# A residual add on GpSimd, one gather later in every step

## The reference

```python
xn = _layernorm(x, axis=-1)
x = x + _L0_attn_ref(xn, Wq, Wk, Wv, Wo, We) + _L0_ffn_ref(xn, gate_w, w1, b1, w2, b2)

# _L0_attn_ref: ctx = X @ We.T ; influence = ctx @ ctx.T
scores = jnp.einsum('bqhd,bkhd->bhqk', Q, K) * SCALE + 0.1 * influence[:, None]
out = softmax(scores) @ V, heads joined, then @ Wo.T

# _L0_ffn_ref: probabilities by softmax over 8 logits, top 2 taken
h = gelu(w1[e] @ x + b1[e])
y = w2[e] @ h + b2[e]
out = sum over the 2 experts of y * prob
```

## Time and profile before

| | us |
|---|---|
| median of 3 runs | 795.96 |
| lowest and highest run | 795.24 and 799.38 |
| the profiled execution's own time | 795.8 |
| its span, from first to last instruction | 794.1 |
| second attention in the span | about 552 to the end |

### The profile page before, as it was taken

One profiled execution on the slowest core, in us unless ns is written; L12 is line 12 of the kernel. 1 busy time (PEld: TensorE's weight loads), 2 busy tenths in 40 slices (PEclk: granted clock), 3 DMA queues, 4 the chain that ended last, 5 costly groups with the idle time before them and its releaser, 6 DMA issues.

```text
span 794.1 us, 25470 instructions
## 1 busy us (share of the span) xinstructions
PE 694.2 (87%) x8124; PEld 454.6 (57%) x8124; DVE 657.5 (83%) x1182; ACT 527.1 (66%) x1128; POOL 536.6 (68%) x600
## 2 busy tenths in 40 slices
PE   0477889898899897889999999999899999999984
PEld 0363344444444453479999999998444444544442
DVE  8989868887778785879999999999888888888851
ACT  2591566776667676767777777777677767667663
POOL 9660656666466565137777777876777777877885
PEclk9995789999999998999999999999999999999998
DMA  9669545666465564643333333332667776776652
GB/s 263 247 206 306 141 118 147 158 165 163 116 169 156 160 170 118 161 102 96 90 100 92 95 94 92 94 96 69 146 154 159 169 161 153 171 160 161 145 108 54
DMA packets 132631, 113.64 MB, mean 143 GB/s; under 512 B 16448, under 2 KB 121152, under 8 KB 132544
## 3 DMA queue, kind: packets, MB, share of 16 engines
q1 hardware_dynamic: 116144, 90.89, 42.9%
q0 software_dynamic: 15360, 16.86, 10.6%
q10 hardware_dynamic: 1040, 4.76, 1.6%
HBM read 64.86 MB, written 47.33 MB: 141 GB/s over the span
## 4 chain that ended last, share of the span: by engine, by line
PE 48%; POOL 19%; issue 13%; DVE 9%; SPq 4%; ACT 3%; another core or an unknown queue 2%; DMA 1%; POOLq 0%; ACTq 0%; DVEq 0%
PE bank L1245 12%; PE mx L1234 12%; POOL rows L600 11%; PE bank L1126 9%; POOL rows L597 7%; PE bank L1103 6%; DVE mx L946 4%; PE mx L1138 3%; ACT A L705 2%; PE bank L1226 2%; DVE A L786 2%; SPq L313 1%; POOL x L586 1%; PE bank L1023 1%
## 5 line engine op out<-in xcount | busy, mean ns | idle before, releaser
L705 ACT ACTIVATE A<-bank 128x512 f32<-128x512 f32 x512 | 279.2, 599 | 102.9 <-PE bank L1126 91.7
L946 DVE TENSOR_REDUCE mx<-mx 128x4 f16<-128x1024 f32 x256 | 301.1, 1206 | 51.3 <-PE mx L1138 27.9
L1126 PE MATMUL bank<-stack 113*128 113x256 f16 x1024 | 179.0, 282 | 37.1 <-ACT A L705 21.6
L549 POOL DMA_INDIRECT slots_x<-rows,pos x128 | 124.0, 969 | 86.6 <-PE bank L1126 65.1
L1126 PEld LDWEIGHTS bank<-stack 113*128 113x128 f16 x1024 | 70.0, 98 | 158.3 <-issue 81.4
L751 ACT ACTIVATE rows<-mx,b 128x256 f32<-128x256 f32 x288 | 121.7, 480 | 57.7 <-PE mx L1234 57.7
L563 POOL TENSOR_SCALAR rows<-rows,slot_p 128x128 f32<-128x128 f32 x144 | 127.1, 892 | 43.3 <-DVE rows L999 43.3
L1103 PE MATMUL bank<-A,V 128*32 128x256 f32 x2048 | 141.2, 394 | 0.0
L600 POOL DMA_INDIRECT rows<-slots_y,pos x64 | 99.2, 1550 | 22.7 <-PE bank L1126 12.0
L1245 PE MATMUL bank<-w,rows 128*128 x1728 | 109.3, 219 | 0.0
L993 DVE TENSOR_TENSOR rows<-rows 128x512 f16<-128x512 f32 x144 | 102.9, 715 | 4.9
(11 more groups left out here) (142 smaller groups left out, 675.9 us busy)
## 6 DMA issues: line engine op xcount, KB each, us to landing
stack<-ctx_rest SPq DMA_DIRECT2D x64, 256.0 KB
stack<-qk_dram SPq DMA_DIRECT2D x128, 96.0 KB
rows<-slots_x SPq DMA_DIRECT2D x72, 129.0 KB, 2.3
slots_y<-rows SPq DMA_DIRECT2D x72, 128.0 KB, 1.8
qk_dram<-hi_qk SPq DMA_DIRECT2D x64, 128.0 KB
stack<-ctx_high SPq DMA_DIRECT2D x128, 64.0 KB
slots_x<-A ACTq DMA_DIRECT2D x1, 4644.0 KB, 19.9
w_stage<-in_w SPq DMA_DIRECT2D x8, 512.0 KB
```

Of the source, the lines that this page charges most:

```text
L549: pool.indirect_dma_start(slots_x, bass.IndirectOffsetOnAxis(pos[j][:, t:t + 1], 0), rows[:, t, :].bitcast(F32), None).then_inc(s_scat, 16)
L705: act.activation(A[:, n % NA, :, :].rearrange("p h s -> p (h s)"), EX[n % 2][:, :], ACT.Exp, scale=SCALE).then_inc(s_xp, 1)
L946: dve.tensor_reduce(mx[:, a, 8 * qt:8 * qt + 8].rearrange("q (i e w) -> q i e w", i=2, e=2)[:, :, g % 2], MX[u % 2][:, :].rearrange("q (i ...
L1126: mm = pe.matmul(EX[p][:, i * S:(i + 1) * S], stack[0:SHIFT + 1, par, h, 1, c * P:(c + 1) * P], stack[0:SHIFT + 1, par, h, 0, :], start=Tr ...
```

## The change

add_experts(n - 1) is issued behind m = 3 instead of behind m = 2. Nothing else differs, and the lists of the four other engines are the same instruction for instruction.

```diff
-                    if m == 2 and n:
+                    if m == 3 and n:
                         add_experts(n - 1)
```

## The result

| | before | changed |
|---|---|---|
| median, 11 runs of each on one chip | 795.24 | 799.68 |
| lowest and highest | 793.34 and 801.64 | 798.36 and 804.07 |
| ratio, 95% interval | | 1.0050 [1.0031, 1.0069] |
| the profiled execution and its span | 795.8, 794.1 | 799.94, 798.2 |

The forecast was 796.4 us in a range of 795.1 to 798.5; the time lies 1.2 us above the range. On another chip the same pair gave 799.23 against 796.28 (12 and 17 runs), ratio 1.0041 [1.0021, 1.0061].

A forecast was written before the change was run, and what follows sets the result against it. Bound: the issue of GpSimd's last DMA plus a fixed 8.5 us tail. Gather 3's wait for TensorE adds 0.42 us, carry from earlier steps 0, other terms 0: 795.96 + 0.4 = 796.4 us, range 795.1 to 798.5.

The follow-up runs named there:

- burst: Kernel before, with the second and third gather of each step waiting for no more of s_ex than the first: 819.90 against 802.27 us, ratio 1.0202.

## What to carry to other kernels

A prediction that holds one engine's times fixed while another's DMAs move rests on an assumption of its own, even where no semaphore links the two; give that a rival with a price. In the trace, look for engines that wait for different results and are released within some tenths of a us, and for waits whose releaser can't be named: such time isn't in any engine's work. Such a mark is no measure, though: the kernel before had its late releases with TensorE named, and only a count of long waits on a chip without them showed that. And where the effect may lie in the chip, put the runs that are to be compared beside the kernel before on a chip that shows it: one question here had to be asked again for that reason, and one stayed unanswered.

## What the runs showed of the hardware

- Late releases of 1 to 2.5 us at several engines at once, tied to when GpSimd issues indirect DMAs: the unnamed waits are 1.8 us in sum before, up to 48.9 in a burst, and none on two chips; waits of ACT of 1 us and more in the second attention are 36 before and 3 on a chip without the effect. SBUF — State Buffer, of the Trainium skill, says in its opening lines that the engines' ports and the DMA ports of SBUF can't contend with each other. These runs don't contradict it, since they don't show the place; but they show that the time at which transfers are issued can cost compute all the same: 17.6 and 16.8 us for one and the same set of transfers with the gathers 1 and 2 allowed earlier.
- The same kernel takes 795 to 802 us on some chips and 756.5 on two others, with the difference in the attention stages (scatters of the first attention 229 and 200 to 202 us; second attention 241 us before and 232 with the add behind m = 1; expert tiles 203 on both).
- The row of GpSimd's add begins up to 0.57 us before the accumulating DMA ahead of it ends, and is that much longer (1.85 to 1.88 us for 1.28); behind a plain gather it begins 0.02 us after its end.
